# Rotary projections without the half-swapped weight products; VectorE swaps the halves of the partitions; the values product issued in one piece

## The reference, cut to what matters

```python
def _apply_rope(x, cos, sin):
    d = x.shape[-1]
    x1, x2 = (x[..., :d // 2], x[..., d // 2:])
    rot = jnp.concatenate([-x2, x1], axis=-1)
    return x * cos + rot * sin
...
cq = _gelu(x @ wq + bq)
q_c = cq @ wqc + bqc
q_r = x @ wqr + bqr
ckv = _gelu(x @ wkv + bkv)
k_r = x @ wkr + bkr
k_c = ckv @ wkc + bkc
v = (ckv @ wv + bv).reshape(b, s, H, HD).transpose(0, 2, 1, 3)
q_r = _apply_rope(q_r, cos, sin)
k_r = _apply_rope(k_r, cos, sin)
q = _gelu(jnp.concatenate([q_c, q_r], axis=-1)).reshape(b, s, H, HD).transpose(0, 2, 1, 3)
k = _gelu(jnp.concatenate([k_c, k_r], axis=-1)).reshape(b, s, H, HD).transpose(0, 2, 1, 3)
scores = jnp.einsum('bhqd,bhkd->bhqk', q, k) * scale
...
attn = jax.nn.softmax(scores, axis=-1)
out = jnp.einsum('bhqk,bhkd->bhqd', attn, v)
return out.transpose(0, 2, 1, 3).reshape(b, s, E) @ wo + bo
```

## Time and profile before

| | us |
|---|---|
| median of three executions | 1025.22 |
| lowest, highest | 1022.64, 1028.29 |
| the profiled execution, its own time | 1020.24 |
| its span, first to last instruction | 1018.2 |
| first run of self attentions, about | 334 to 512 |
| second run, about | 852 to 931 |

### The profile page before, as it was taken

How to read it: one execution, slowest core, us unless ns; L and a number is a source line. 1 busy time by engine, 2 the same in 40 slices (tenths; PEclk the granted TensorE clock), 3 DMA queues, 4 the chain that set the end, 5 groups by cost and what they waited for, 6 DMA issues and landing times.

```text
span 1018.2 us, 26020 instructions
## 1 busy us (share of the span) xinstructions
PE 975.1 (96%) x10833; PEld 832.8 (82%) x10833; DVE 601.0 (59%) x1419; ACT 450.9 (44%) x907; POOL 168.5 (17%) x357
## 2 busy tenths in 40 slices
PE   5999999999999989999889999997999999999998
PEld 5888888888888867778669999996888888777887
DVE  5745644555332656567788787777677663465242
ACT  3333333333333365654226666663444444574241
POOL 2312212112112113323430000004112000111000
PEclk9999999999999999999979999998999999999999
DMA  9400000000000092000049999922111002000000
GB/s 318 136 12 22 1 23 21 1 2 1 2 1 1 10 369 117 2 13 13 22 104 319 374 365 378 357 91 61 36 55 43 3 2 75 2 2 1 1 21 22
DMA packets 64196, 86.47 MB, mean 85 GB/s; under 512 B 8968, under 2 KB 55504, under 8 KB 63568
## 3 DMA queue, kind: packets, MB, share of 16 engines
q1 hardware_dynamic: 62544, 80.61, 23.4%
q0 software_dynamic: 1536, 4.20, 1.3%
HBM read 75.62 MB, written 9.18 MB: 83 GB/s over the span
## 4 chain that ended last, share of the span: by engine, by line
PE 87%; DVE 7%; ACT 4%; issue 2%; DMA 0%; POOL 0%; DVEq 0%; ACTq 0%; POOLq 0%
PE ps L630 9%; PE ps L645 9%; PE ps L2334 7%; PE ps L2347 6%; PE ps L2673 6%; PE ps L1445 3%; PE ps L614 3%; PE ps L662 3%; PE ps L1160 3%; PE ps L584 3%; PE ps L682 3%; PE ps L1544 2%; PE ps L1527 2%; PE ps L1085 2%; PE ps L1484 2%; PE ps L1095 2%
## 5 line engine op out<-in xcount | busy, mean ns | idle before, releaser
L2334 PE MATMUL ps<-moe_xT,ew 128*128 128x128 f32 x736 | 91.0, 278 | 2.2 <-issue 1.2
L773 ACT ACTIVATE x0pT<-ps 128x512 f32<-128x512 f32 x64 | 38.3, 598 | 123.6 <-PE ps L645 123.6
L2334 PEld LDWEIGHTS ps<-moe_xT,ew 128*128 128x128 f32 x736 | 87.2, 194 | 3.4 <-DVE moe_xT L2423 1.9
L383 POOL TENSOR_TENSOR rn_tmp<-rn_cur,eps 128x1 f32<-128x1 f32 x48 | 13.2, 274 | 348.4 <-DVE rn_cur L377 348.2
L888 DVE TENSOR_TENSOR x0A_lo<-ps,x0A_hi 128x512 fp32r<-128x512 f32 x64 | 41.1, 685 | 31.7 <-ACT x0A_hi L764 31.7
L2673 PE MATMUL ps<-f,ffw 128*128 128x512 f32 x256 | 59.1, 390 | 0.8 <-issue 0.6
L2347 PE MATMUL ps<-ew_2hi,eh_hi 128*128 128x256 f32 x184 | 55.4, 301 | 1.9 <-DVE eh_lo L2476 1.5
L2673 PEld LDWEIGHTS ps<-f,ffw 128*128 128x128 f32 x256 | 47.8, 188 | 11.5 <-issue 0.9
L2283 DVE TENSOR_TENSOR ew_2lo<-ew,ew_2hi 128x1024 fp32r<-128x1024 f32 x46 | 55.9, 1216 | 0.0
L2533 POOL DMA_INDIRECT yg<-moe_out,slot x16 | 16.3, 1016 | 234.7 <-DMA moe_out<-moe_y 163.7
L630 PE MATMUL ps<-x0wv_hi,x0cT_hi 128*128 128x512 f32 x128 | 52.8, 413 | 0.6 <-DVE x0A_lo L888 0.6
(11 more groups left out here) (333 smaller groups left out, 2460.0 us busy)
## 6 DMA issues: line engine op xcount, KB each, us to landing
ew<-L_ffn_W_dram SPq DMA_DIRECT2D x46, 1024.0 KB, 8.0
x0cin<-ctx_dram SPq DMA_DIRECT2D x8, 512.0 KB, 4.1
x1cin<-ctx_dram SPq DMA_DIRECT2D x8, 512.0 KB, 4.0
moe_out<-moe_y SPq DMA_DIRECT2D x23, 128.0 KB, 4.5
xg<-moe_in SPq DMA_DIRECT2D x21, 128.0 KB, 8.1
moe_in<-padneg SPq DMA_DIRECT2D x2, 1024.0 KB, 13.4
maskrow<-mask_BxS_ik_dram SPq DMA_DIRECT2D x2, 1024.0 KB, 7.8
x0wk<-L_xattn_Wkv_dram SPq DMA_DIRECT2D x1, 1024.0 KB, 7.1
```

The source lines that it names most:

```text
L773: nc.scalar.activation(g.pT[:, u, :], ps[:, S_BANK[u % 2], :], ACT.Exp, scale=64.0 ** -0.5).then_inc(C0.exp, 1)
L2334: last = nc.tensor.matmul(ps[:, n % 3, j * BT:j * BT + BT], ew1[b % NW][:, i, f * P:f * P + P], xT[b % 2][:, i, :], start=(i == 0), stop=( ...
```

## The change

`fill_rope` makes two products per tile instead of four, the ones with the plain weights. `rotate` reads each of them with one operation on all 128 partitions (cosine) and two on 64 partitions (sine): the first reads partitions 0 to 63 of the product, the bias and the table and writes partitions 64 to 127 of the result, the second reads the upper half and writes the lower. The table's sign is that of the half read, so the pairs are subtracted instead of added. The two swapped weights are no longer loaded, two DMAs of 128 KB at the start. `fill_pv` is one call with all 16 products, at the place of the second of the two calls.

```diff
             def fill_rope(n):
                 RS.wait_free(pe, n, "rope")
-                for i in range(4):
+                for i in range(2):
...
-            def fill_pv(n, half):
-
-                if half == 0:
-                    pe.wait_ge(SA.exp, n + 1)
-                    pe.wait_ge(SA.v_frame, 3 * span + 3)
-                    RS.wait_emptied(pe, n, "v")
-                    RS.wait_free(pe, n, "pv")
-                for j in range(4 * half, 4 * half + 4):
+            def fill_pv(n):
+
+                pe.wait_ge(SA.exp, n + 1)
+                pe.wait_ge(SA.v_frame, 3 * span + 3)
+                RS.wait_emptied(pe, n, "v")
+                RS.wait_free(pe, n, "pv")
+                for j in range(8):
...
-                if half == 1:
-                    last.then_inc(SA.fill, 1)
+                last.then_inc(SA.fill, 1)
...
                     if n != lo + 1:
                         fill_rope(n + 2)
-                    if back:
-                        fill_pv(n - 1, 0)
                     fill_qkc(n + 2)
                     if back:
-                        fill_pv(n - 1, 1)
+                        fill_pv(n - 1)
...
                     if front and not begun:
                         fill_qk(n + 2, "k")
-                    if back:
-                        fill_pv(n - 1, 0)
                     if front and not begun:
                         fill_qk(n + 2, "q")
                     if span == 0 and hi - 2 <= n <= hi:
                         RS.wait_free(pe, n - 1, "T")
                         keep_clock(RS.bank(n - 1, "T"), 3 if n == hi - 2 else 2)
                     if back:
-                        fill_pv(n - 1, 1)
+                        fill_pv(n - 1)
...
-                for i, (bias, tab) in enumerate((("bqr", cos), ("bqs", sin), ("bkr", cos), ("bks", sin))):
-                    last = nc.vector.scalar_tensor_tensor(g.rope[:, i, :], RS.bank(n, "rope")[:, i * P:i * P + P], vec(bias), tab, ALU.add, ALU.mult)
+                for i, bias in enumerate(("bqr", "bkr")):
+                    src = RS.bank(n, "rope")[:, i * P:i * P + P]
+                    nc.vector.scalar_tensor_tensor(g.rope[:, 2 * i, :], src, vec(bias), cos, ALU.add, ALU.mult)
+                    for half in range(2):
+                        here, there = slice(64 * half, 64 * half + 64), slice(64 - 64 * half, 128 - 64 * half)
+                        last = nc.vector.scalar_tensor_tensor(g.rope[there, 2 * i + 1, :], src[here, :], vec(bias)[here, :], sin[here, :], ALU.add, ALU.mult)
                 last.then_inc(SA.by_dve, 1)
                 RS.wait_emptied(dve, n, "rope")
-                nc.vector.tensor_tensor(g.rope[:, 0, :], g.rope[:, 0, :], g.rope[:, 1, :], ALU.add)
-                nc.vector.tensor_tensor(g.rope[:, 2, :], g.rope[:, 2, :], g.rope[:, 3, :], ALU.add).then_inc(SA.roped, 1)
+                nc.vector.tensor_tensor(g.rope[:, 0, :], g.rope[:, 0, :], g.rope[:, 1, :], ALU.subtract)
+                nc.vector.tensor_tensor(g.rope[:, 2, :], g.rope[:, 2, :], g.rope[:, 3, :], ALU.subtract).then_inc(SA.roped, 1)
...
-            for i, w in enumerate(("wqr", "wqr_swapped", "wkr", "wkr_swapped")):
+            for i, w in enumerate(("wqr", "wkr")):
                 whole(w_mla[:, :, P + P * i:2 * P + P * i], weight("L0_attn_" + w), ld["mla"])
```

More of the change, by code:

```diff
@@ L1590, in pe_self @@
                 pe.wait_ge(SA.tables, 2)
-                pe.wait_ge(ld["mla"], 160)
+                pe.wait_ge(ld["mla"], 128)
                 pe.wait_ge(ld["sq0"], 64)
```

## The result

| | before | after |
|---|---|---|
| median of 17 executions each, us | 1024.17 | 1031.88 |
| lowest, highest | 1021.91, 1028.63 | 1027.30, 1041.46 |
| ratio of the two, 95% interval | | 1.0076, 1.0056 to 1.0096 |
| the profiled execution, its own time | 1020.24 | 1036.73 |
| its span, mean granted clock | 1018.2, 0.990 | 1035.0, 0.967 |

The change costs 0.76%, 7.7 us. The forecast was 1026.0 us, no difference; the measured median lies 0.4 us above the range. The profiled execution is one of the slower ones of 17, so its profile shows the loss larger than the median does. Among the 17 the time roughly follows the clock: 1027.3 us at 0.980, 1031.9 at 0.970, 1041.5 at 0.964.

The account below looks back on a forecast made before the run. TensorE was taken to bound the kernel, with 87% of the chain. Rotary +2.9, values product -4.0 - 0.6 + 0.5 and clock +2.0 gave +0.8 us on the 1025.2 median: 1026.0 us, range 1019.8 to 1031.5.

Parts of the forecast that it names:

- Part 1: Rotary products on TensorE: each of eight tiles loses 0.9 us, 7.1 in all; together with part 2, +2.9 us.
- part 2: Rotation on VectorE: six operations instead of four take 2.1 us, 1.0 more per rotation.
- Its other end: Rotation on VectorE: if the six operations overlap, 0.5 us more per rotation, making rotary products and rotation together -1.0 us.
- Part 3: Values product in one piece: 0.3 us less per step, -4.0 in 13 steps, -0.6 in steps 22 to 24, +0.5 in 14 to 16.
- Part 4: Loads at the start: two of 128 KB fewer, worth nothing because DMA has no share of the chain.
- Part 5: TensorE's clock in steps 0 and 1: more likely than not falls once to half, costing +2.0 us.
- The last rival: Step 15: without the first half TensorE idles 1.8 us, the clock falls and 6 us are lost, 1032 us; chance 0.15.
- half operations do not overlap: Rival on VectorE's rotation: the half operations do overlap, -5.1 us, 1020.1 us; chance 0.12.
- one piece is cheaper: Rival on the values product: one piece is not cheaper, 4.6 us of gain are missing, 1030 us; chance 0.06.
- the clock did not hold: Rival on TensorE's clock: it holds, -1.2 us, 1024.0 us; chance 0.25.
- the rotation in 2.1 us: Sign on VectorE: six operations take about 2.1 us, ends of one at starts of the next.
- about 1 us idle before the transpose: Sign in step 2 on TensorE: about 1 us idle before the transpose, 0.2 us more up to the output projection.

Follow-up runs that it names:

- pv_split_end: Kernel before with the values product in one piece, except in steps 14 to 16, where halves stay around the clock-keeping products; 1018.21 us.
- no_swap: after_split_end with the two half-partition operations replaced by one on all partitions, leaving the swap out of the computation; 1013.39 us.
- filled_3: after_split_end plus three clock-keeping products with unused results in TensorE's gap in steps 1, 2, 4, 6 and 8; 1019.89 us.
- after_split_end: The whole change, but in steps 14 to 16 the values product stays in two halves around the clock-keeping products; 1029.32 us.
- six_full: no_swap with a third full-partition operation each for q and k, so six without a change of partitions; 1017.57 us.
- pv_only: Kernel before with only the values product of the change, in one piece, and the rotation as before; 1019.76 us.
- rope_only: Kernel before with only the rotary products and rotation of the change, the values product as before; 1034.05 us.
- grouped: after_split_end with the six rotation operations reordered: both full ones, then both reading partitions 0 to 63, then both reading 64 to 127; 1023.94 us.
- change_filled_3: The change itself plus three clock-keeping products in the gaps of steps 1, 2, 4, 6 and 8; 1020.03 us.
- filled: after_split_end plus five clock-keeping products in TensorE's gap in steps 1, 2, 4, 6 and 8; 1026.08 us.

## Why the prediction was wrong, point by point

Taken apart by differences against before: the values product -5.6 (pv_split_end), the fewer rotary products -4.4 (no_swap against it), the longer rotation at held clock +7.0 (filled_3 against no_swap), the clock in the mla steps +8.5 (after_split_end against filled_3). Together +5.5, as they must, being differences in a row; the last three cross two series each and are good to some 3 to 4 us, and of these only the last two are clear of noise. The change itself has +7.7, 2.2 more; it differs from after_split_end in steps 14 to 16 alone, but those 2.2 are not clear of noise.

- *Part 1 and part 2, +2.9*: right in size, as far as can be told. Measured -4.4 + 7.0 = **+2.6** by the medians (4.9 by the ratios, 4.4 by the transpose of step 9 in the profiles of filled_3 and pv_split_end), of which up to 0.17 us in each of five steps is the overshoot of the filler. The two steps at full clock above agree: 19.19 us for 19.35, where the sums say +0.2 for the mla step and -0.3 for the other. The price of 1.0 per rotation, from the copies on 64 partitions, was 1.03. Its other end (-1.0 with 0.5 per rotation) can be read off six_full: 5.3 against 5.6, +0.3 with one fall in it.
- *Part 3, -4.0 and -0.6, and +0.5 in steps 14 to 16*: right in price and sum, 0.32 per step for a forecast 0.31, and **-4.1** as a whole (pv_only; 5.3 by its ratio). The sum is partly luck. With the old rotation the mla steps gain too: pv_only's transposes are 4.7 us earlier by step 13, where 8 steps of 0.31 make 2.5. In its profile 1.1 us of that is gone again between steps 16 and 17, in stages that the change does not touch.
- *Part 4, loads, nothing*: nothing in any run speaks against it.
- *Part 5, the clock, +2.0*: **this step failed.** "I think it more likely than not that the clock falls once here." It fell in the mla steps up to five times and cost **8.5 us** there (after_split_end against filled_3). Two things went wrong in it. I looked for the fall in steps 0 and 1 only. And I wrote for the other steps "The 0.9 us saved in the products stand as idle time before the transpose", about 1 us of gap. The same sums give more: 0.19 that stood there, 0.9 from the rotary products, 0.3 from the values product in one piece (which I had booked as "in the mla steps it changes nothing"; rope_only, without it, has 1.59), and 0.4 for the attention output that comes later, 1.8; measured 1.91. Both causes of the gap were in my text, each priced on the path, and never added up as a gap. By the gap in these steps, one profile each: 0.73 (no_swap) no fall, 1.26 (six_full) one, 1.59 (rope_only) five, 1.60 (grouped) four, 1.91 (after_split_end) four. So from 0.73 to 1.6 us the falls went from none to four or five, and a still longer gap brought no more; the gap of about 1 us that I had written down lies between. The kernel before had one hint: its own fall at 513 comes behind 1.55 us of idle, longer than the one us that I read from the earlier trace rows. TensorE's timeline of the kernel before:

```profile
512.14 0.18 PE L1567 MATMUL ps<-picked,before 128*128 128x8 bf16 x1 [1.55 <-DVE picked_to L2254]
```

- *The last rival, the clock falls again in step 15, 1032 us, 0.15*: its number is the measured time, and the fall of step 15 is in the profile. But it is only a small part of the loss in the median: putting the halves back in steps 14 to 16 gave 2.2 us (after_split_end), and holding the clock in the mla steps alone took 9.9 us off, more than the whole 7.7. The time was right by luck, the place was not.
- *The other rivals*: half operations do not overlap as the change orders them (grouped shows that they can); one piece is cheaper; the clock did not hold.
- *What would show it*: of the signs named, the rotation in 2.1 us, step 18 shorter by 0.3 and 0.50 of clock in 360 to 380 came true; the transpose of step 1 came 1.7 us later in rope_only, for 2.0 in steps 0 and 1; that of step 15 lost 0.5 against the one before it in pv_only, as forecast; "about 1 us idle before the transpose" was 1.91, and that was the sign to have worked through.

The Trainium skill ("TensorE: Matmul & The Clock Gate", section "A second HAM failure mode: psum-queue depth-cycling") describes an engine whose frequent short pauses between groups of products make the gate swing between its two levels. The trace agrees: no gap of TensorE in the mla steps of the kernel after is longer than 1.95 us, and the clock falls five times. I had leaned on the neighbouring section, on long pauses, and on the earlier trace rows, a whole us of idle, and so looked for one large fall rather than for several small ones.

## What to carry to other kernels

When an edit takes products off TensorE and makes the engine that it waits for slower, add up the gap itself, not only what either side does to the path, and do it in every step where they meet; here four gaps of 1.7 to 1.9 us, in a change worth about 3 us on the path, cost some 8 us of clock. The clock can be bought back cheaply: products whose result nobody reads, laid into the gap and hardly longer than it, made this kernel 0.8% faster. That is also a quick test of whether a loss is clock or path. When operations work on parts of the partitions, put those that start at the same partitions next to each other.

## What the runs showed of the hardware that was not expected

- Half-partition operations that read one half and write the other cost no more than full ones (0.26 us start to start) beside a neighbour with the same partitions, and 0.36 beside one with others. The order of six of them was worth 4.9 us of 1029, at most 2.5 of it on VectorE.
- Gaps of TensorE of at most 1.95 us were enough for five falls of the clock in steps 1 to 9. The length of one gap does not decide by itself: of the four gaps of 1.91 to 1.95 us in the profile after, the one in step 6 was followed by no fall, and the fall of 447 to 452 came behind gaps of 0.72 and 0.58; a gap of 1.80 us in step 15 went with a long fall in the change and with none there in change_filled_3 and pv_only. A gap of 1.41 or 1.42 us in step 1, at the same place in six kernels, was followed by a fall in the profiles of three (the change, filled, change_filled_3) and by none before the next gaps in the other three (after_split_end, filled_3, rope_only). What decides it stays open.
- A low stretch lasts: from 505 to 528 in the kernel after TensorE was at 1.2 GHz while busy for 21.69 of 23 us, and in the kernel before from 513 to 526. In pv_only the whole of steps 1 to 16 ran at 1.00.
